# Rows added into zeroed expert queues, and row numbers worked out on GpSimd

## What is computed

```python
x = x + attention(layernorm(x), ctx, ctx)      # 16 heads of 8; each query sees 65 keys
xf = layernorm(x).reshape(4096, 128)
k_probs, k_idx = top_k(softmax(xf @ router_w.T), 2)      # two experts of eight for each token
rank = position of the (token, choice) pair in its expert's queue
keep = rank < capacity                                   # capacity 1281
buf  = zeros(E, capacity, H).at[expert, slot].add(row if keep else 0)
h    = silu(buf @ w1);  out_buf = h @ w2                 # 128 -> 512 -> 128, for each expert
result = x + xf_reshaped + sum over the two choices of out_buf[expert, slot] * gate
```

## Time and profile before

| | us |
|---|---|
| median of 3 runs (lowest, highest) | 610.28 (607.23, 615.94) |
| the profiled execution's own time | 609.36 |
| its span, first to last instruction | 607.6 |
| PE, DVE, ACT, POOL busy | 432.4, 330.0, 264.6, 323.0 |
| L1280, 88 DMAs, busy on POOL | 137.8 |
| L1197, 64 DMAs, busy on POOL | 64.5 |

### The profile page before, as it was taken

One profiled execution on the slowest core, in us unless ns is written; L12 is line 12 of the kernel. 1 busy time (PEld: TensorE's weight loads), 2 busy tenths in 40 slices (PEclk: granted clock), 3 DMA queues, 4 the chain that ended last, 5 costly groups with the idle time before them and its releaser, 6 DMA issues.

```text
span 607.6 us, 16667 instructions
## 1 busy us (share of the span) xinstructions
PE 432.4 (71%) x5554; PEld 336.1 (55%) x5554; DVE 330.0 (54%) x1039; ACT 264.6 (44%) x578; POOL 323.0 (53%) x341
## 2 busy tenths in 40 slices
PE   3265569687797789778877886149977987987710
PEld 2144356565575566556655665038866866866600
DVE  4772357675685568567756545326654564463310
ACT  1112235443553345344444443138856665665400
POOL 5521124445644654465446425601877877877874
PEclk9775789987988898899889878559979888888955
DMA  9887567555554554565435311232454454443432
GB/s 179 223 214 175 149 169 188 150 144 136 154 143 126 154 153 125 132 168 152 119 112 162 104 31 45 81 126 80 70 106 82 60 105 88 53 70 27 36 27 21
DMA packets 82448, 70.45 MB, mean 116 GB/s; under 512 B 9632, under 2 KB 68257, under 8 KB 81888
## 3 DMA queue, kind: packets, MB, share of 16 engines
q1 hardware_dynamic: 68576, 60.36, 38.1%
q0 software_dynamic: 13824, 9.47, 12.1%
HBM read 39.11 MB, written 31.00 MB: 115 GB/s over the span
## 4 chain that ended last, share of the span: by engine, by line
PE 31%; issue 19%; POOL 19%; SPq 9%; DMA 7%; another core or an unknown queue 6%; ACT 4%; DVE 2%; POOLq 0%; ACTq 0%; DVEq 0%
PE bank L450 28%; POOL out L1280 14%; DMA maxima_scratch<-maxT 2%; SPq L349 2%; POOL queues L1197 2%; SPq L347 2%; SPq L329 1%; SPq L334 1%; ACT probs L738 1%; DMA k_scratch<-parts 1%; DVE ys L1136 1%; ACT xcT L769 1%; DMA q_pack<-maxima_scratch 1%; DMA cst<-in_consts 1%
## 5 line engine op out<-in xcount | busy, mean ns | idle before, releaser
L1280 POOL DMA_INDIRECT out<-ys,row_token x88 | 137.8, 1566 | 58.9 <-issue 26.9
L869 DVE TENSOR_REDUCE maxima<-bank 128x4 f32<-128x512 f32 x128 | 87.7, 687 | 107.0 <-remote 56.4
L738 ACT ACTIVATE probs<-bank 128x512 f32<-128x512 f32 x128 | 76.4, 597 | 104.1 <-PE bank L450 60.4
L450 PE MATMUL bank<-xTp,w1p 128*128 128x512 f32 (+1 forms) x288 | 76.1, 422 | 9.0 <-DVE xTp L1112 9.0
L1197 POOL DMA_INDIRECT queues<-rows,index x64 | 64.5, 1008 | 19.7 <-issue 18.7
L450 PE MATMUL bank<-q_pack,k_pack 128*128 128x64 bf16 x1024 | 56.5, 202 | 19.6 <-DMA q_pack<-maxima_scratch 17.4
L450 PE MATMUL bank<-k_pack,q_pack 128*64 128x128 bf16 x1024 | 58.5, 243 | 16.7 <-DMA k_pack<-k_scratch 16.1
L450 PEld LDWEIGHTS bank<-xTp,w1p 128*128 128x128 f32 x288 | 56.8, 224 | 21.8 <-issue 6.7
L1159 DVE TENSOR_TENSOR hidp<-hid,hidp 128x512 fp32r<-128x512 f32 (+1 forms) x96 | 56.9, 604 | 22.1 <-ACT hidp L844 17.2
L1242 POOL TENSOR_TENSOR qk<-straight,turned 128x512 f32<-128x512 f32 x16 | 22.3, 1392 | 86.2 <-issue 65.3
L450 PE MATMUL bank<-probs,v_sb 128*32 128x64 f32 x2048 | 60.6, 237 | 9.5 <-issue 7.0
(11 more groups left out here) (100 smaller groups left out, 659.5 us busy)
## 6 DMA issues: line engine op xcount, KB each, us to landing
k_pack<-k_scratch SPq DMA_DIRECT2D x64, 192.0 KB, 3.7
q_pack<-q_scratch SPq DMA_DIRECT2D x64, 128.0 KB, 3.1
queues<-empty SPq DMA_DIRECT2D x8, 682.5 KB, 7.4
xs<-queues SPq DMA_DIRECT2D x8, 650.0 KB
q_scratch<-parts SPq DMA_DIRECT2D x16, 192.0 KB
k_scratch<-parts SPq DMA_DIRECT2D x16, 192.0 KB
xin<-in_x SPq DMA_DIRECT2D x16, 128.0 KB, 3.1
cin<-in_ctx SPq DMA_DIRECT2D x16, 128.0 KB, 3.5
```

The lines of the kernel that those rows point to most:

```text
L450: return nc.tensor.matmul(o, l, r, start=start, stop=stop)
L738: nc.scalar.activation(probs[u % 2][:], bb[u % 2][:], ACT.Exp).then_inc(S["prob_s"], 1)
L869: v.reduce_max(maxima[par][:, 4 * hg:4 * hg + 4, i2], ab[u % 2][:].rearrange("p (h c) -> p h c", c=P), AX).then_inc(S["max_s"], 1)
L1280: g.indirect_dma_start(out, bass.IndirectOffsetOnAxis(ap=row_token[par][0:n, t:t + 1], axis=0), ys[s][0:n, col // P, :], None, compute_op= ...
```

## The change

Three things are changed together. The scatters into the queues (L1197) now add to what is there, with `compute_op=ALU.add` in place of the bounds check; a row past the capacity goes to a place of its own behind the queues, for which the tensor is longer and VectorE takes a minimum with `nowhere`, which it moves on by 512 in each batch. The tile `empty` is all zeros, and a tag is the token's number plus one, as a float, so that zero means that a place is empty. In the expert stage GpSimd makes an expert's row numbers from the tags: where the tag is zero it puts the number of a spare row (`spare`), and then subtracts one; these are six instructions more for each expert, and each needs the one before it.

```diff
-    queues = nc.dram_tensor("queues", [EXPERTS * QUEUE, ROW], F32).ap()
+    queues = nc.dram_tensor("queues", [EXPERTS * QUEUE + 2 * ALL, ROW], F32).ap()
...
-                        v.reduce_sum(index[par][:], picked[:].rearrange("p s t e -> p (s t) e"), AX
-                                     ).then_inc(S["gate_s"], 1)
+                        done(v.reduce_sum(sums[:], picked[:].rearrange("p s t e -> p (s t) e"), AX))
+                        need(10)
+                        v.tensor_tensor(index[par][:], sums[:], nowhere[:], ALU.min).then_inc(S["gate_s"], 1)
+                    after(dve, "gate_s", 3, j)
+                    done(v.tensor_scalar(nowhere[:], nowhere[:], float(2 * TOKENS), None, ALU.add))
...
                     g.indirect_dma_start(queues, bass.IndirectOffsetOnAxis(ap=index[par][:, n:n + 1], axis=0),
-                                         rows[par][:, n // TILES, n % TILES, :], None,
-                                         bounds_check=EXPERTS * QUEUE - 1, oob_is_err=False).then_inc(S[f"scattered{par}"], 16)
+                                         rows[par][:, n // TILES, n % TILES, :], None, compute_op=ALU.add
+                                         ).then_inc(S[f"scattered{par}"], 16)
...
-                    g.tensor_copy(rows[par][:, :, :, DIM + 1].bitcast(I32),
+                    g.tensor_copy(rows[par][:, :, :, DIM + 1],
                                   tok[:].unsqueeze(1).to_broadcast([P, 2, TILES])).then_inc(S["tok_s"], 1)
...
                     g.tensor_copy(row_gate[par][0:n, a:b], xs[par][0:n, a:b, DIM]).then_inc(S["tags_s"], 1)
-                    g.tensor_copy(row_token[par][0:n, a:b], xs[par][0:n, a:b, DIM + 1].bitcast(I32)
-                                  ).then_inc(S["tags_s"], 1)
+                    pool.wait_ge(S["spare_made"], 2)
+                    g.tensor_scalar(vacant[0:n, a:b], xs[par][0:n, a:b, DIM + 1], 0.0, None, ALU.is_equal
+                                    ).then_inc(S["vacant_s"], 1)
+                    pool.wait_ge(S["vacant_s"], e * 6 + 3 * (a // 10) + 1)
+                    apart(pool, "past_pool")
+                    g.tensor_tensor(vacant[0:n, a:b], vacant[0:n, a:b], spare[0:n, a:b], ALU.mult).then_inc(S["vacant_s"], 1)
+                    pool.wait_ge(S["vacant_s"], e * 6 + 3 * (a // 10) + 2)
+                    apart(pool, "past_pool")
+                    g.tensor_tensor(vacant[0:n, a:b], vacant[0:n, a:b], xs[par][0:n, a:b, DIM + 1], ALU.add
+                                    ).then_inc(S["vacant_s"], 1)
+                    pool.wait_ge(S["vacant_s"], e * 6 + 3 * (a // 10) + 3)
+                    apart(pool, "past_pool")
+                    g.tensor_scalar(row_token[par][0:n, a:b], vacant[0:n, a:b], -1.0, None, ALU.add).then_inc(S["tags_s"], 1)
```

## The result

The changed kernel takes 605.28 us (median of 4 runs, 600.27 to 607.17) where the kernel before takes 611.03 on the same chip (4 runs, 607.23 to 615.94): a ratio of 0.990, 95% interval 0.985 to 0.994. That is 6 us faster, where 54 slower was forecast. Two things have to be explained: why the attention stage became faster, and what became of the costs. A third came up on the way: on other chips of the same type the kernel before takes 562 to 564 us, while the changed one, timed on one of them, still takes 604.6. There the change costs 7.3%.

What follows compares the result with a forecast made beforehand. GpSimd's scatter bursts were taken to halt the attention stage, and GpSimd to pace the expert stage: 609.36 + 29.0 + 6.0 + 17.6 + 1.0 = 662.96, plus 0.9, so 664 us, 8.8% slower; range 615 to 695.

Steps and rivals of the forecast that it cites:

- The step that failed: Attention stage: other engines idle until the burst of four scatters ends, so 13 bursts each pay 2.23 us, 29.0 us.
- The standstill: Attention stage: TensorE, ScalarE and VectorE stop until the scatter burst ends; ScalarE idle 4.38 us, VectorE 4.76, without a linking semaphore.
- Burst and scatter: Attention stage: adding scatter near 1566 ns against 1008, burst of four 7.17 us against 4.94, 2.23 us more.
- third rival: Queue scatters: 520-byte adding rows are dearer, cut in two pieces; up to 764 us, 690 with a quarter; chance 0.13.
- The 13 steps: Attention stage: 13 bursts in which scores run, each 2.23 us longer, 29.0 us in all.
- The last three bursts: End of attention stage, no scores running, GpSimd on the path: 2.2, 1.6 and 2.2 us more, sum 6.0.
- Row numbers: Expert stage, GpSimd's dependent chain: 2.51 us later for each of 7 experts, 17.6 us; bounds 9.9 and 24.5.
- The 1.10 us from `ys` to the DMA: Expert stage: taken as the cost of starting an expert's first output DMA, so it moves by all of 2.51 us.
- VectorE's minimum: Attention stage: two dependent VectorE instructions, about 0.4 us a step; 1.0 us taken, between 0 and 6.4.
- The first, the standstill gone: Attention stage: only plain scatters stop the engines, so 3.4 x 12 = 41 us saved, 594 us; chance 0.18.
- Its allowance of 1.0 us a step for GpSimd's longer burst: Attention stage: of 4.4 us shed per step, 1 us kept for VectorE waiting on a 2.23 us longer burst.
- The second, the longer burst hidden: Attention stage: engines idle for another reason, burst's end only coincides, so the 29.0 falls away; 635 us, chance 0.15.

Runs made afterwards that it cites:

- r3: Changed kernel with plain scatters and a bounds check that never drops a row; 585.07 us, 1.032 of the kernel before (564.41 on that chip).
- r4: Kernel before without the bounds check on its plain scatters, with VectorE's minimum and `nowhere`; 563.78 us, ratio 1.000 (kernel before 564.41 on that chip).

## Why the prediction was wrong

**The step that failed** is "If the other engines go on standing still until the burst ends, each of the bursts in which scores run pays this in full ... 13 x 2.23 = 29.0 us". The standstill was read rightly as the largest unexplained cost of the stage, but it is not a property of a burst: on chips like the first it comes with plain scatters issued back to back, in the kernel before and in the changed one, and neither with adding scatters nor with a fill between. So what was forecast at +29.0 us for the thirteen bursts came out as 32.0 us less. The text named this as what would make it most wrong, and gave it 0.18. The evidence for it was in the old trace (adding DMAs back to back in the expert stage held nobody) and I set it aside because the matmuls there are others.

The Trainium skill ("Trainium Architecture — The Big Picture", What this means for kernel authors) has the engines as independent processors that block each other only through a semaphore. On quick chips that is what the traces show: no profile there has a wait "remote". The three profiles of plain bursts on the other kind show waits of 3.1 to 5.2 us in the rows above, for signals of TensorE's. The Trainium skill ("Perfetto Trace Analysis", Summary: the profiler window per engine type) lists the passing on of a semaphore among what is hidden from TensorE's profiled time. That agrees with how it looks here, a wait whose releaser is "remote" and whose cause no row carries. But where in that path the signal was held, or whether TensorE itself was held, as its own stops with the burst moved suggest, no run shows.

**Term by term, on the first chip:**
- Burst and scatter: 2.23 us longer forecast, 2.25 measured; 1566 ns, measured 1577. The dearer rows of the third rival don't exist.
- The 13 steps: +29.0 forecast; the eleven steps between the second burst and the thirteenth took 192.5 us instead of 221.0, 28.5 less, and with the start 32.0 less.
- The last three bursts: 6.0 forecast. From the thirteenth burst's start to the end of the last 41.4 us instead of 34.7, so 6.6 more; on a quick chip 9.1.
- Row numbers: 17.6 forecast, in bounds of 9.9 and 24.5. The gaps are about 2.8 us longer, 7 of them 19.5; a chain's step is 0.36 to 0.40 us as taken from `tok`, but the first compare runs beside the end of the last DMA (0.96 us to the next start) and one conversion waits 0.51. The 1.10 us from `ys` to the DMA was indeed a start's cost: it is still 1.13 (423.16 to 424.29). The other 3.1 of the stage's 22.5 are 35 ns on each of the 88 output DMAs, 1601 against 1566. I had no term for that. It is there with plain scatters as well (r3: 1599), and not with the row numbers on VectorE (1574 and 1581), nor in the variants of the kernel before (1563 to 1590); why is open.
- VectorE's minimum: 1.0 forecast, 0 measured (r4), behind 3 us of slack.

**The rivals.** The first, the standstill gone, was the right one on the first chip, and its 594 was 11 low: it credited 41 us where 32 came, and took over the 17.6. Its allowance of 1.0 us a step for GpSimd's longer burst was nearly right: a step became 3.15 us shorter, of a wait of 4.4. But it counted twelve such steps at 3.4, where eleven gave 28.5 in all, 2.6 each, and the start 3.5: the 4.4 that it started from was one row's, and ScalarE's waits were 43.6 us in 14, 3.1 each. The second, the longer burst hidden, had 635: it would have needed the standstill to stay. On a quick chip there is no standstill to gain or to lose, and the costs stand alone. Read from the two profiles there, they are 562.6 + 19.5 (row numbers) + 3.1 (output DMAs) + 19.4 (longer bursts: 7.1 in the eleven steps, 9.1 in the last bursts, the rest at the start) = 604.6, and 604.56 was measured. That is a balance made afterwards and no forecast; the prediction's own terms without the 29.0 would have given 562.6 + 6.0 + 17.6 + 1.0 = 587, with the longer bursts 13 too low.

**Open:** what differs between the chips, whether it is TensorE's signals or TensorE's own progress that plain scatters hold and why adding ones don't, and whether the distance of their starts or the instruction between them decides.

## What to carry to other kernels

A wait whose releaser the profile can't name is not a cost that scales with the work beside it: before it is multiplied by anything, ask which property of that work it hangs on, and look for the same work elsewhere in the trace without it. An engine that is busy half the time can still be close to setting the pace of one stage; its slack in a step (here 1.2 us) decides how much of added work is seen, and a dependent chain of small instructions in front of a waiting engine is seen in full. Where a kernel's time may differ by chip, compare candidates on several: here the fill between plain scatters (568 and 572) and adding scatters with VectorE's row numbers (584 and 583) are nearly the same on both kinds, while the kernel before takes 562 on one, as good as any, and 607 on the other.

## What was not expected of the hardware

- The same program takes 562 to 564 us on four chips and 607 to 611 on at least three others, and nearly all of the difference is the 12 to 14 standstills of three engines while GpSimd issues plain indirect scatters 1.27 us apart (waits of 3.1 to 5.2 us in the rows shown, steps of 20.6 instead of 16.4).
- 0.55 us of other work on GpSimd between two such scatters, or adding scatters in their place (1.54 us each instead of 0.97), removes them.
- With the plain burst moved, TensorE too stops during it, up to 1.00 us at a time in the burst shown, without a wait that the profile can name.
- GpSimd started the next instruction 0.53 us ahead of an adding scatter's end (232.19 against 232.72), so that `base` and the copy behind it show 1.24 and 0.74 us for 0.71 and 0.22 of work.
